# Second FFN of a macaron block: another order of turning, routing and projecting, and reciprocals spread by a float32r product

## What is computed

```
x = x + 0.5 * ffn(layernorm(x), Wr, We)
x = x + attention(layernorm(x), Wq, bq, Wk, bk, Wv, bv, Wo, bo)
x = x + 0.5 * ffn(layernorm(x), Wr, We)
```

## Time and profile before

| | us |
|---|---|
| median of 3 runs | 6545.29 |
| lowest and highest of them | 6541.36, 6547.69 |
| profiled execution, its own time | 6538.67 |
| its span, first to last instruction | 6536.8 |
| second FFN: first matmul to end of span | 5975.95 to 6536.8 |
| PE, DVE, ACT and POOL busy over the span | 96%, 92%, 73%, 6% |

### The profile page before, as it was taken

The page is one execution under the profiler, slowest core; times in us unless marked ns, Lnnn a source line. Parts: engine busy times, 40 slices in busy tenths (PEclk is TensorE's granted clock), DMA queues, the critical chain, the costliest instruction groups (busy, mean ns, idle before and its releaser), DMA issues. The chain is left out here.

```text
span 6536.8 us, 158115 instructions
## 1 busy us (share of the span) xinstructions
PE 6260.8 (96%) x54288; PEld 2794.2 (43%) x54288; DVE 6022.9 (92%) x6989; ACT 4749.2 (73%) x8697; POOL 378.0 (6%) x604
## 2 busy tenths in 40 slices
PE   7888599999999999999999999999999999998998
PEld 5666433333333333333333333333333333334776
DVE  7888599999999999999999999999999999992776
ACT  2222138888888888888888888888888888885111
POOL 2322300000000000000000000000000000001221
PEclk9999779999999999999999999999999999999999
DMA  2222401010000101010101010101010101000110
GB/s 81 88 91 93 100 11 16 13 17 17 13 16 13 20 10 20 10 20 10 20 10 20 10 22 12 20 10 23 13 16 13 16 13 16 4 20 29 51 46 27
DMA packets 120628, 174.85 MB, mean 27 GB/s; under 512 B 61760, under 2 KB 78672, under 8 KB 116944
## 3 DMA queue, kind: packets, MB, share of 16 engines
q1 hardware_dynamic: 120144, 167.19, 11.2%
HBM read 97.93 MB, written 69.21 MB: 26 GB/s over the span
## 5 line engine op out<-in xcount | busy, mean ns | idle before, releaser
L1020 DVE TENSOR_REDUCE at_mx<-at_m 128x1 f32<-128x1024 f32 x4070 | 4975.9, 1223 | 82.0 <-PE at_m L954 38.3
L995 ACT ACTIVATE at_ex<-at_s 128x512 f32<-128x512 f32 x8192 | 4449.0, 595 | 715.7 <-PE at_s L905 144.6
L905 PE MATMUL at_s<-at_q,at_k 50*128 50x512 f32 x8192 | 2995.5, 444 | 0.0
L884 PE MATMUL at_m<-at_k,at_q 48*128 48x512 f32 x8032 | 2923.9, 443 | 1.0 <-DVE at_mx L1020 1.0
L915 PE MATMUL at_po<-at_ex,at_v 128*32 128x256 f32 x32816 | 2623.6, 391 | 31.7 <-POOL at_v L853 31.7
L884 PEld LDWEIGHTS at_m<-at_k,at_q 48*128 48x128 f32 x8032 | 1183.1, 185 | 1657.1 <-DVE at_mx L1020 1596.8
L915 PEld LDWEIGHTS at_po<-at_ex,at_v 128*32 128x32 f32 x32816 | 646.3, 108 | 1519.0 <-issue 746.4
L905 PEld LDWEIGHTS at_s<-at_q,at_k 50*128 50x128 f32 x8192 | 1211.2, 185 | 42.7 <-ACT at_ex L995 42.3
L299 PE MATMUL fr_ps<-sh_weh,fr_xl 128*128 128x512 f32 x512 | 179.7, 433 | 115.9 <-DVE fr_acc L470 115.9
L859 POOL COPY at_v<-at_vst 128x1024 f32<-128x1024 f32 x16 | 16.7, 1041 | 4557.7 <-DMA at_vst<-v_by_head 4557.7
L1279 PE MATMUL bk_ps<-sh_weh,bk_xl 128*128 128x512 f32 x512 | 169.0, 411 | 23.5 <-DVE bk_acc L1404 23.5
(11 more groups left out here) (169 smaller groups left out, 2802.8 us busy)
## 6 DMA issues: line engine op xcount, KB each, us to landing
at_q<-q_parts SPq DMA_DIRECT2D x96, 256.0 KB, 4.9
at_k<-k_parts SPq DMA_DIRECT2D x96, 256.0 KB, 6.3
q_parts<-fr_parts SPq DMA_DIRECT2D x64, 256.0 KB, 2.2
k_parts<-fr_parts SPq DMA_DIRECT2D x64, 256.0 KB, 2.4
attended<-at_o SPq DMA_DIRECT2D x256, 34.0 KB
fr_x<-in_x SPq DMA_DIRECT2D x16, 512.0 KB, 4.2
after_ffn<-fr_acc SPq DMA_DIRECT2D x16, 512.0 KB, 3.0
v_by_head<-fr_v SPq DMA_DIRECT2D x16, 512.0 KB, 4.1
```

Of the source, the lines that this page charges most:

```text
L884: ins = pe.matmul(pm[w][:, h * QB:(h + 1) * QB], Q[p][rows, base + i * P:base + (i + 1) * P], K[p][rows, c * CW + h * QB:c * CW + (h + 1) ...
L905: pe.matmul(ps[event(t) % NS], K[p][rows, j * P:(j + 1) * P], Q[p][rows, sb_ * QU + g * QB:sb_ * QU + (g + 1) * QB], start=True, stop=True ...
L995: ac.activation(Ex[QUAD * (j % NX) + 2 * g + 1 - half][:, :], ps[event(t) % NS], ACT.Exp)\
L1020: ve.tensor_reduce(out=mx[u][:, i, c:c + 1], in_=first[(v * RED + k) % len(first)][:, 0:CW] if opening else pm[w][:, :], op=ALU.max, axis= ...
```

## The change

In `back_phase` the order of the two engines is another one; no step is added or taken away but for what is said on the reciprocals below.

- PE: tile 0; `spread_out(g+2)`; tile 1; `turn(g+1)`; n8, n9; `router(g+1)`; `project(g+2)`; n10, n11; tile 3; `positions(g+1)`.
- DVE: c0, c1; `statistics(g+1)`; c2, c3; `normal(g+1)`; c4, c5; `normalise_heads(g+2)`; c6 to c9; `pick(g+1)`; in body 0 the inversion of the second batch row's sums; c10 to c13; `odds(g+1)`; c14, c15; `room(g+1)`; `add_residual(g+2)`.

The reciprocals are split into a float32r value (high) and the float32r remainder (low), which are stored one behind the other. `rec` and `spread` so have 32 rows, of which 16 are for the high and 16 for the low parts, and a single float32r matmul spreads their sum. For that DVE copies the constant into a float32r tile once, and for each batch row makes one cast and one subtraction of 128x512 behind the reciprocal. SP stores 16 pieces for each batch row where it stored 8, and PE waits once at its start for DVE's part.

```
-                ve.wait_ge(ahead.s_sum, GB * DMA)
-                ve.reciprocal(ahead.recs[0][:, :], ahead.sums[0][:, :]).then_inc(ahead.s_all, 1)
+                invert_sums(ve, ahead, 0)
...
+def invert_sums(ve, t, b):
+
+    if b == 0:
+        ve.wait_ge(t.s_c, 3 * DMA)
+        ve.tensor_copy(t.spread[:, :], t.spread32[:, :]).then_inc(t.s_all, 1)
+    ve.wait_ge(t.s_sum, (b + 1) * GB * DMA)
+    high, low = t.split[b]
+    ve.reciprocal(t.recs[b][:, :], t.sums[b][:, :]).then_inc(t.s_all, 1)
+    ve.wait_ge(t.s_all, 3 * b + 2)
+    ve.tensor_copy(high[:, :], t.recs[b][:, :]).then_inc(t.s_all, 1)
+    ve.wait_ge(t.s_all, 3 * b + 3)
+    ve.tensor_tensor(low[:, :], t.recs[b][:, :], high[:, :].bitcast(F32), ALU.subtract).then_inc(t.s_all, 1)
...
-    hold(sp, t.s_all, 1, tick)
-    for dst, src in store(t.recs[0], 0):
+    hold(sp, t.s_all, 4, tick)
+    for dst, src in store(t.split[0], 0):
         sp.dma_start(dst, src).then_inc(t.s_rd, DMA)
-    hold(sp, t.s_rd, GB * DMA, tick)
+    hold(sp, t.s_rd, 2 * GB * DMA, tick)
...
                     experts(g, u, 1, 0, NP)
+                    if runs(g, 1):
+                        turn(g + 1)
+                    experts(g, u, 2, 0, NP // 2)
+                    if runs(g, 1):
+                        router(g + 1)
                     if runs(g, 2):
                         project(g + 2)
-                    if runs(g, 1):
-                        turn(g + 1)
-                    experts(g, u, 2, 0, NP // 2)
-                    if runs(g, 1):
-                        router(g + 1)
                     experts(g, u, 2, NP // 2, NP)
...
-                    combine(g, u, it, 0)
+                    combine(g, u, it, 0, 0, E // 2)
+                    if runs(g, 1):
+                        statistics(g + 1, y[1 - u])
+                    combine(g, u, it, 0, E // 2, E)
+                    if runs(g, 1):
+                        normal(g + 1, y[1 - u])
+                    combine(g, u, it, 1, 0, E // 2)
                     if runs(g, 2):
                         normalise_heads(g + 2, u, it + 1)
-                    combine(g, u, it, 1, 0, E // 2)
-                    if runs(g, 1):
-                        statistics(g + 1, y[1 - u])
                     combine(g, u, it, 1, E // 2, E)
-                    if runs(g, 1):
-                        normal(g + 1, y[1 - u])
+                    combine(g, u, it, 2, 0, E // 2)
+                    if runs(g, 1):
+                        pick(g + 1)
                     if isinstance(g, int) and g == 0:
-                        ve.wait_ge(s_sum, 2 * GB * DMA)
-                        ve.reciprocal(recs[1][:, :], sums[1][:, :]).then_inc(s_all, 1)
-                    combine(g, u, it, 2)
-                    if runs(g, 1):
-                        pick(g + 1)
+                        invert_sums(ve, ahead, 1)
+                    combine(g, u, it, 2, E // 2, E)
```

More of the change, by code:

```diff
@@ L102, in sem @@
         return nc.alloc_semaphore(f"bk_{n}")
-    return Ahead([sb(f"at{u}", [P, NC, GT]) for u in range(2)], [sb(f"rec{u}", [H, GT]) for u in range(2)],
-                 [sb(f"x{u}", [P, TG, D]) for u in range(2)], sb("wo", [P, NC, D]), sb("bo", [P, D]), sb("spread", [H, P]),
+    return Ahead([sb(f"at{u}", [P, NC, GT]) for u in range(2)], [sb(f"rec{u}", [2 * H, GT], F32R) for u in range(2)],
+                 [sb(f"x{u}", [P, TG, D]) for u in range(2)], sb("wo", [P, NC, D]), sb("bo", [P, D]), sb("spread32", [2 * H, P]),
+                 sb("spread", [2 * H, P], F32R),
                  [sb(f"sums{b}", [P, H * S // P]) for b in range(B)], [sb(f"recs{b}", [P, H * S // P]) for b in range(B)],
+                 [[sb(f"split{b}{t}", [P, H * S // P], F32R) for t in range(2)] for b in range(B)],
                  *([sem(f"{n}{u}") for u in range(2)] for n in ("at", "rec", "x")),
@@ L1076, in reciprocals @@
     def reciprocals(g):
-        return rec_dram.rearrange("h b s -> h (b s)")[:, bass.ds(g * GT, GT)]
+        return rec_dram.rearrange("t h b s -> (t h) (b s)")[:, bass.ds(g * GT, GT)]
     def pieces(dram, tile, b):
@@ L1082, in pieces, with parts @@
                 for k in range(GB)]
-    return attended, residual, reciprocals, lambda tile, b: pieces(sums, tile, b), lambda tile, b: pieces(rec_dram, tile, b)
+    def parts(tiles, b):
+        return [p for t in range(2)
+                for p in pieces(rec_dram[t:t + 1, :, :, :].rearrange("t h b s -> (t h) b s"), tiles[t].bitcast(F32), b)]
+    return attended, residual, reciprocals, lambda tile, b: pieces(sums, tile, b), parts
+def invert_sums(ve, t, b):
[9 more added lines that the diff above has]
+    ve.tensor_tensor(low[:, :], t.recs[b][:, :], high[:, :].bitcast(F32), ALU.subtract).then_inc(t.s_all, 1)
 def fetch_ahead(sp, t, sources, constants):
@@ L1091, in fetch_ahead @@
         sp.dma_start(dst, src).then_inc(t.s_sum, DMA)
-    for dst, src in zip((t.spread[:, :], t.wo[:, :, :], t.bo[:, :]), constants):
+    for dst, src in zip((t.spread32[:, :], t.wo[:, :, :], t.bo[:, :]), constants):
         sp.dma_start(dst, src).then_inc(t.s_c, DMA)
@@ L1132, in back_phase @@
         ident, wr, before, ones, order, weh, wel = shared
-        at, rec, xg, wo, bo_sb, spread, sums, recs, s_at, s_rec, s_x, s_c, s_sum, s_all, s_rd = ahead
+        at, rec, xg, wo, bo_sb, spread32, spread, sums, recs, split, s_at, s_rec, s_x, s_c, s_sum, s_all, s_rd = ahead
         keep = sb("keep", [P, NG])
@@ L1211, in body @@
                     if isinstance(g, int) and g == 1:
-                        hold(sp, s_all, 2, s_tick)
-                        for dst, src in recs_of(recs[1], 1):
+                        hold(sp, s_all, 7, s_tick)
+                        for dst, src in recs_of(split[1], 1):
                             sp.dma_start(dst, src).then_inc(s_rd, DMA)
-                        hold(sp, s_rd, 2 * GB * DMA, s_tick)
+                        hold(sp, s_rd, 4 * GB * DMA, s_tick)
                     hold(sp, s_ac, g * STEPS + STEPS, s_tick)
@@ L1284, in _ @@
                 pe.wait_ge(s_c, 3 * DMA)
+                pe.wait_ge(s_all, 4)
                 spread_out(0, 0, 0)
@@ L1297, in body @@
                     experts(g, u, 1, 0, NP)
-                    if runs(g, 2):
-                        project(g + 2)
                     if runs(g, 1):
@@ L1304, in body @@
                         router(g + 1)
+                    if runs(g, 2):
+                        project(g + 2)
                     experts(g, u, 2, NP // 2, NP)
@@ L1566, in program @@
     att = dram("attended", (HD + 1, H, B, S))
-    recs = dram("reciprocals", (H, B, S))
+    recs = dram("reciprocals", (2, H, B, S))
     rows = dram("max_rows", (B * H * S // 2048, P, 32))
@@ L1598, in shape_constants @@
         "order": np.tile(np.arange(E, 0, -1, dtype=np.float32), (P, 1)),
-        "spread": np.tile(np.eye(H, dtype=np.float32), (1, P // H)),
+        "spread": np.tile(np.eye(H, dtype=np.float32), (2, P // H)),
         "cos": table(np.cos),
```

8 lines of the change are left out of this document (4 added, 4 removed).

## The result

| | before | after |
|---|---|---|
| median, us | 6543.32 (4 runs, 6531.59 to 6547.69) | 6493.22 (4 runs, 6487.16 to 6494.35) |
| span of the profiled execution, us | 6536.8 | 6485.3 |
| first matmul of the second FFN, us from the start | 5975.95 | 5969.15 |
| second FFN, from there to the end of the span | 560.85 | 516.15 |

The ratio is 0.9924, with a 95% interval from 0.9907 to 0.9942: the time is shorter, by 50 us in the medians and 51.5 in the two profiled spans. 43.9 were forecast. Of the 51.5 us, 44.7 lie in the second FFN; the other 6.8 lie ahead of it.

The account below looks back on a forecast made before the run. PE bounds the groups, with holes made by order. Savings of 1.5 (prologue), 1.6, 2.3, 23.5 (ten loop groups), 4.7, 2.3 and 8.0 sum to 43.9 us: 6545.3 becomes 6501.4, range 6493 to 6512 (chance 0.75).

Parts of the forecast that it names:

- What bounds it: Loop groups: PE carries them, with order-made holes ended by VectorE, 1.34 us ahead of turning and 1.60 ahead of n15.
- The check that the prediction names: Loop groups: the same counting of start times on the old order gives its holes where the rows have them.
- A group of the loop: Second FFN's loop: each group goes from 33.31 to 30.96 us, 2.35 less; ten groups save 23.5.
- The float32r product at nothing: PE's spreading in the groups: 0.7 to 0.8 us shorter, hidden by the hole before n7, so worth nothing.
- The prologue: Ahead of the groups: the cheaper spreading, run at the lower clock with VectorE waiting, saves 1.5 us (bounds 0 to 1.5).
- The inversions: Batch row 0, end of attention: costs nothing. Row 1, behind `pick` in group 0: 4.5 us long, costing 1 (0 to 2.2).
- Group 12: First group behind the loop: VectorE's stand falls on c6 or so, 36.72 becomes 32.0 us (31.0 to 34.4).
- Group 14: Group without projecting: no long wait ahead of turning, POOL's delay covered; 35.50 becomes 27.5 us, saving 8.0.
- (b): Rival: the hole before n7 lowers the clock in each group; 13 groups give back 23 us, 6525; chance 0.08.
- (c): Rival: VectorE's unpaused run from c15 to c4 is longer than its pieces add up to; slower result, chance 0.04.
- (d): Rival: routing waiting for ACT and n15 for c13 take 2.5 us a group, giving back 32; 6534; chance 0.06.
- (a): Rival: holes before n5 and n7 close, PE is the bound at 29.2 us a group; 23 us more saved, 6478; chance 0.07.

Follow-up runs that it names:

- the repetition: The changed kernel run once more, nothing altered; median 6499.3 us, ratio 0.9930 to the kernel before.
- e1: Kernel before with only the new orders on PE and VectorE, float32 spreading kept; 30.77 us a loop group, median 6503.1 us, ratio 0.9939.
- e5: Changed kernel with `normal` moved behind c4 and `normalise_heads` behind c6; 29.40 us a loop group, median 6477.9 us, ratio 0.9908 to the kernel before.
- e2: Kernel before with only the float32r spreading and its inversions, both orders old; 32.67 to 32.73 us a loop group, median 6538.0 us, ratio 0.9997.
- e4: Changed kernel with PE's order put back to the old one; 31.60 us a loop group, median 6520.9 us, ratio 0.9965 to the kernel before.
- e6: As e5 but with the float32 spreading of the kernel before; 29.95 us a loop group, median 6480.8 us, ratio 0.9907 to the kernel before.
- e3: Changed kernel with VectorE's order put back to the old one; 37.54 us a loop group, median 6596.8 us, ratio 1.0088 to the kernel before.

## Why the prediction was right

The forecast of 6501.4 lies 8 us above the first median and 2 above the repetition's. Against the second FFN alone, which the change is in, 43.9 stand against 44.7 and 43.8. That is closer than the terms are: by the profile pair the ten groups gave 2.1 us more than forecast and groups 0, 1, 13 and 14 together 0.7 more, the prologue 1.0 and group 12 0.7 less, and these errors cancel to within 1 us. So much of the closeness is luck. The mechanism is not: the orders were tried singly and together.

- **What bounds it.** Right: order, not work. With the same work (e1, where no step differs but in place) 30.77 instead of 33.31. The check that the prediction names, the same counting on the old order, is not worked out in it. What tests the counting are the experiments: 29.4 to 29.6 for 29.40 in e5, but 32.85 for 32.70 in e2 (on the wrong path) and 31.3 for 31.60 in e4.
- **A group of the loop.** 30.96 was counted, 30.76 measured; ten of them gave 25.6 for 23.5. The idle time was said to be 1.6 ahead of n7 and up to 0.3 ahead of n5; it is 1.18 and none. The term that was mis-sized is VectorE's run to c4: 10.93 behind n0 by the sum, 10.79 by the rows (6193.30 less 6182.51), and projecting behind routing takes 3.35 (6201.23 to 6204.58) instead of 3.45.
- **The float32r product at nothing.** Shown by e1, and its 0.6 with the hole closed by e5 and e6, where the sum had 0.8 for that case. In its place PE takes 0.43, where the sum had 0.23 and 0.1 to 0.2.
- **The prologue.** The one term that failed as a whole: 1.5 less was forecast, 28.9 became 28.5, and 29.1 in the repetition. In all profiles it is 28.7 to 29.2 us long with the float32 product (three) and 28.5 to 29.1 with the other (nine), so the term is nothing that the profiles show. The step itself was right (the spreading 0.76 busy for 2.04, and `normalise_heads` 1.3 us sooner behind it), but projecting gave it back. The windows over the first two projections, before and then after (columns as in the earlier trace rows):

```profile
5979.44:5985.05 5.61, 5.61 (x16) 4.30 (x16) 0.00 (x0) 0.00 (x0) 2.76 (x4) 0.66 0.65 199
5998.97:6004.88 5.91, 5.91 (x18) 4.71 (x18) 2.43 (x13) 1.49 (x2) 1.40 (x7) 0.59 0.41 134
```

```profile
5971.36:5977.52 6.16, 6.15 (x16) 4.68 (x16) 0.00 (x0) 0.00 (x0) 3.05 (x8) 0.60 0.56 159
5991.43:5997.61 6.18, 6.18 (x17) 4.91 (x18) 2.43 (x13) 1.49 (x2) 2.09 (x11) 0.56 0.21 73
```

They take 6.16 and 6.18 us for 5.61 and 5.91, at mean clocks of 0.60 and 0.56 for 0.66 and 0.59: PE has worked less ahead of them (0.76 us instead of 2.04 ahead of the first), and more of them runs at 1.2 GHz. The other profiles agree: the first projecting takes 5.45 to 5.77 us in the three, 6.16 to 6.60 in the nine. I had carried the durations over as they were. The second spreading of the prologue is 1.28 shorter too (0.79 for 2.07), and routing behind it then waits 1.44 us for ACT's copy, where it waited 0.15.

- **The inversions.** 4.5 were counted behind `pick`, and in group 0 the rows have 3.35, 0.43 and 0.69:

```profile
6018.71 3.35 DVE L1100 RECIPROCAL bk_recs<-bk_sums 128x512 f32<-128x512 f32 x1
6022.10 0.43 DVE L1102 CAST bk_split<-bk_recs 128x512 fp32r<-128x512 f32 x1
6022.56 0.69 DVE L1104 TENSOR_TENSOR bk_split<-bk_recs,bk_split 128x512 fp32r<-128x512 f32 x1
```

The group got 1.84 shorter, 1.6 by the sum. The cast and the subtraction cost it 0.8 (31.24 against e1's 30.44, which has the reciprocal at the same place without them); the whole inversion was counted as 1. Batch row 0 cost nothing, as forecast: the 16 stores took 8.67 us, where 7.4 were counted, and the loads behind them were issued 73 us ahead of the FFN's first matmul (5896.31 and 5969.15). The cast takes 0.43, where the sum had 0.4 and the prediction's estimate by two elements a cycle had 0.3. The Trainium skill (VectorE: DVE Perf Modes, Specifications) gives VectorE's clock as 0.96 GHz. An estimate from that page, at one element a cycle for the subtraction and two for the cast: the subtraction's 512 elements are 0.53 of its 0.69 us, the rest is 0.16, and 0.27 and 0.16 are the cast's 0.43. So these rows agree with the rule, and my estimate had left out the fixed part.
- **Group 12.** 32.0 forecast, 32.76 measured. VectorE's stand came ahead of `normalise_heads`, one step from the c6 that had been named, and 2.35 long, so that c6 was late for n9 (1.72 us of idle time there), which "free by 1.5" had left out.
- **Group 14.** 27.5 forecast, 27.25 measured; the clock stays at 1.00 there, and POOL's late `route` costs nothing. It is late as before: 2.7 us behind the end of `pick` in the old trace (6504.40 to 6507.12), where the prediction has 2.5, and 2.8 in the new.
- **The rivals.** (b) did not come, but its mechanism is real: at 4.79 us a group in e3 the clock falls in each. (c) and (d) did not come: VectorE's run is 0.14 shorter than its pieces, not longer, and neither ACT nor c13 holds PE. (a) is what e5 made of the kernel.

## What to carry to other kernels

When two engines hand work to each other in an order written out by hand, write the starting times of both down for one round, from the old trace, and move steps until the holes are gone: here that gave 30.96 for 30.76, and 29.4 to 29.6 for 29.40 in the next step, and within 0.3 in e2 and e4. Then check in the rows which wait the number came from: in e2 it was near for another path than the one counted. A cheaper instruction is worth what the next wait behind it leaves: the same product was worth 0, 0.55 and 0.6 us a group in three orders. Judge a change of a late stage by the length of its own rounds, which here repeats to some hundredths of a us, not by medians over a program whose early part scatters by 19.

## What was not expected of the hardware

VectorE stood for 1.2 to 2.9 us, with nothing that the trace shows to wait for, at a place behind the loop that moved with the number of instructions ahead. Where it hit a combine that PE needed, it cost 5.8 us, since the clock fell too (group 12 of e5, 35.16 against 29.40), and 246 empty instructions in an idle stretch took that away; what the stand is stays open. And a matmul's duration must not be carried from one point of a cold start to another: the same projection took 5.45 to 5.77 us behind one product and 6.16 to 6.60 behind a shorter one.
